# Routing of an attention and mixture-of-experts layer: counts by matmul from the picks, gates from sorted logits, a new order of steps, scatters waited for by the users of their buffers

## The chip, the cores and the metric

The kernel runs on one core of one Trainium2 chip. The metric is the device time of one execution in microseconds. A core has TensorE (PE, matmuls; PEld are its weight loads), VectorE (DVE), ScalarE (ACT), GpSimd (POOL) and SyncE (SP, here only a queue that issues transfers), which run their own instruction streams and meet at semaphores.

## The reference, cut to what matters

```python
x = layernorm(x + attention(x, W_K, W_Q, W_V, W_O))     # x: 2048 x 512, 16 heads of 128
x = layernorm(x + ffn(x, ...))

def ffn(x, gate_w, w1, w2, w3, sw1, sw2, sw3):          # 64 experts, 352 wide, top 6, capacity 128
    logits = x @ gate_w.T
    scores = softmax(logits)
    gate_vals, idx = top_k(scores, 6)
    fe = idx.reshape(-1); ft = repeat(arange(N), 6)     # choices in order of tokens
    onehot = fe[:, None] == arange(64)[None, :]
    pos = cumsum(onehot, axis=0) - 1  taken at fe       # place within its expert
    keep = pos < 128                                    # over capacity: dropped
    ...                                                 # rows gathered by (expert, pos)
    h = silu(xe @ w1.T) * (xe @ w3.T);  ye = h @ w2.T
    routed = sum over the 6 choices of ye * gate_val * keep
    z = (silu(x @ sw1.T) * (x @ sw3.T)) @ sw2.T         # shared expert
    return routed + z
```

## The kernel before, in words

The kernel has three parts, one after the other. `attention` works on pairs of heads. `route_and_experts` first goes through 16 tiles of 128 tokens (the routing loop), then through the experts. `combine` does the last layernorm. The change is in the routing loop and in the few units that follow it (the lead).

Each engine has its own `step(i, k)` of the routing loop, k from 0 to 15, and three tiles are in flight. In step k TensorE projects tile k with the output weights (`project`, 16 heads by three matmuls of 512 columns into `o_ps`), turns tile k-1 (`turn_x1`, four transposes into `t_ps`), counts the choices of tile k-2 (`counts`, into `c_ps`) and makes the logits of tile k-1 (`logits`, into `l_ps`). `LATE = (12, 14)` says that the transposes come after 12 heads and the counts after 14. VectorE in step k adds the residual and normalises tile k-1 (`normalise`), picks the experts of tile k-2 from its logits (`choose`), splits the heads' output of tile k+1 into a high and a low part (`split_z`), makes gates (`route_gates`), splits the turned tile k-1 (`split_x1T`) and works out the rows in the experts' buffers (`places`). ScalarE does the square root, the exponentials, the high parts, and in its step also a piece of the shared expert's weights (`split_shared`). GpSimd, after `placed`, sends the 128 rows of a tile to the six chosen experts by six indirect transfers (`scatter`), waits for them all to land, and only then subtracts the low part of a shared weight piece (`split_shared`) and issues the load of the next (`load_shared`). SyncE loads the heads' output of tile k+2 into the one buffer `z_raw` once `z_lo` of tile k+1 is made.

Normalised rows live in four buffers `x1` (`NB = 4`), with the token number, the chosen experts and the gates in their last 15 columns; slots in two. `normalise` of tile k waits for the scatters of tile k-4, `places` of tile k for those of tile k-2, both by `rows_left`, which GpSimd raises.

After the loop come eight lead units of the shared expert (`lead_up`, `lead_down`), between which the last two tiles are counted and placed. SyncE waits for all scatters before it loads the first expert's rows. A `done(i, k)` is the count a semaphore has once tile k is through; `link` chains the small VectorE steps by waits on a semaphore.

Of the kernel before, what the change touches and what calls it, by code (L numbers as in the profile page):

```python
# [7 lines left out]
P = 128  # L8
# [42 lines left out]
NB = 4  # L51
# [639 lines left out]
def route_and_experts(nc, z_dram, w_o, gate_w, x_rows, w13, w2, s13, s2, sums_dram, x1T_parts, gathered_x):  # L691
# [4 lines left out]
    LATE = (12, 14)  # L696
# [75 lines left out]
    with ExitStack() as ctx:  # L772
# [23 lines left out]
        with ExitStack() as first:  # L796
# [8 lines left out]
            token = sb("token", [P, TILES], I32, first)  # L805
# [9 lines left out]
            top_e = sb("top_e", [P, 8], stack=first)  # L815
            idx = sb("idx", [P, 8], U32, first)
            pick = sb("pick", [P, TOPK, EXPERTS], stack=first)
            pick_pos = sb("pick_pos", [P, TOPK, EXPERTS], stack=first)
            chosen = sb("chosen", [P, EXPERTS], stack=first)
            chosen_bf = sb("chosen_bf", [P, EXPERTS], BF16, first)  # L820
            count = sb("count", [P, EXPERTS], stack=first)
            pos_all = sb("pos_all", [P, EXPERTS], stack=first)
# [7 lines left out]
            ones_bf = sb("ones_bf", [P, P], BF16, first)  # L830
# [26 lines left out]
        with ExitStack() as first:  # L857
            o_ps = ps("o_ps", [P, 2, DM], stack=first)
            t_ps = ps("t_ps", [P, DT * P], stack=first)
            l_ps = ps("l_ps", [P, EXPERTS], stack=first)  # L860
            c_ps = ps("c_ps", [P, 2, EXPERTS], stack=first)
# [42 lines left out]
        l_read = sem("l_read")  # L904
        exp_ready = sem("exp_ready")
# [4 lines left out]
        moved = sem("moved")  # L910
        rows_left = sem("rows_left")
# [29 lines left out]
        LN_STEPS = 9  # L941
        CHOOSE_STEPS, GATE_STEPS = 6, 4
        ROUTE_STEPS = CHOOSE_STEPS + GATE_STEPS + 5
# [9 lines left out]
        def lead_turn(v):  # L953

            return NT - (LEAD - 1) + v

# [22 lines left out]
        def _(pool):  # L979
# [3 lines left out]
            nc.gpsimd.iota(token[:], pattern=[[P, TILES]], base=0, channel_multiplier=1).then_inc(pool_const, 1)  # L983
            pool.wait_ge(pool_step, 2)
# [4 lines left out]
                                    base=0, pattern=[[1, P]], channel_multiplier=-1).then_inc(pool_const, 1)  # L989
            nc.gpsimd.iota(mine_i[:], pattern=[[1, NE]], base=0, channel_multiplier=0).then_inc(pool_const, 1)  # L990
# [81 lines left out]
        def _(sp):  # L1072
# [88 lines left out]
            sp.wait_ge(rows_left, TILES)  # L1161
# [869 lines left out]
```

## Time and profile before

| what | value |
|---|---|
| median of 3 runs | 2573.56 us (2564.14 to 2576.12) |
| the profiled execution's own time | 2573.61 us |
| its span | 2571.8 us |
| TensorE busy | 2444.0 us, 95% |
| VectorE busy | 1778.3 us, 69% |
| ScalarE busy | 1423.4 us, 55% |
| GpSimd busy | 339.3 us, 13% |
| mean granted TensorE clock | 0.983 |

The span runs from the first to the last instruction. The shares are means over attention, routing loop, experts and final layernorm, which have different limits. The routing loop takes about the stretch from 1636 to 1869 us, the lead to about 1907 us. A row of the windows view gives start and end of a stretch and its length, the busy time (and count of instructions) of PE, PEld, DVE, ACT and POOL in it, then TensorE's granted clock as a share of 2.4 GHz, the DMA share and GB/s.

### The profile page before, as it was taken

The numbers are of one execution on the slowest core, as the hardware profiler recorded it, in microseconds if no ns is written. First come the engines' busy times: TensorE is split into PE (matmuls) and PEld (weight loads), VectorE is DVE, ScalarE is ACT, GpSimd is POOL, SyncE is SP. The second block draws the span as 40 slices with busy tenths as digits, with TensorE's granted clock in tenths as the row PEclk, the third lists the DMA queues.
The fourth block names the chain that finished last, engine by engine and source line by source line (L and its number), as shares of the span: only waits on it lengthen the run. The fifth ranks groups of instructions, "written<-read, shape, count | busy, mean of one in ns | idle before, by whom it ended". The sixth has DMA issues, their size and how long they took to land. (4 is left out here: it accounts for less than half of the span.)

```text
span 2571.8 us, 40617 instructions
## 1 busy us (share of the span) xinstructions
PE 2444.0 (95%) x14048; PEld 2115.2 (82%) x14048; DVE 1778.3 (69%) x3802; ACT 1423.4 (55%) x3183; POOL 339.3 (13%) x349
## 2 busy tenths in 40 slices
PE   6999999999999999999999999798899999999992
PEld 5888888888888888888888887677689898888992
DVE  4666666566566567567567657588868888788885
ACT  3555555455455456456446446444437777677771
POOL 0000000000000000000000000155541121212121
PEclk9999999999999999999999999899999999999996
DMA  6411411421421330431421321577659999999995
GB/s 260 132 62 56 139 58 60 134 62 48 134 71 28 130 99 24 125 104 28 126 89 42 104 67 30 195 250 265 221 149 315 297 300 314 284 296 310 310 303 153
DMA packets 193419, 396.99 MB, mean 154 GB/s; under 512 B 23673, under 2 KB 73209, under 8 KB 182976
## 3 DMA queue, kind: packets, MB, share of 16 engines
q1 hardware_dynamic: 163456, 330.69, 38.2%
q0 software_dynamic: 27456, 59.51, 10.0%
q10 hardware_dynamic: 2304, 4.20, 0.4%
q8 instruction: 113, 1.85, 0.3%
q14 instruction: 90, 0.74, 0.1%
HBM read 296.45 MB, written 106.48 MB: 157 GB/s over the span
## 5 line engine op out<-in xcount | busy, mean ns | idle before, releaser
L428 ACT ACTIVATE pT_hi<-turned 128x512 fp32r<-128x512 f32 (+3 forms) x640 | 334.1, 535 | 270.7 <-PE turned L638 268.2
L417 ACT ACTIVATE probs<-bank,neg_max 128x512 f32<-128x512 f32 (+3 forms) x640 | 396.6, 626 | 109.5 <-DVE neg_max L506 104.5
L512 DVE TENSOR_TENSOR pT_lo<-turned,pT_hi 128x512 fp32r<-128x512 f32 (+3 forms) x640 | 377.6, 603 | 75.0 <-ACT pT_hi L428 71.5
L498 DVE TENSOR_REDUCE max_part<-bank 128x1 f32<-128x512 f32 (+2 forms) x576 | 345.4, 620 | 95.9 <-PE bank L621 83.9
L608 PE MATMUL bank<-x_sb,w_hi 128*128 128x512 f32 x1024 | 323.9, 398 | 20.0 <-ACT ident_bf L393 13.3
L638 PE MATMUL turned<-ident,probs 128*128 128x128 f32 x2176 | 329.2, 273 | 0.1
L638 PEld LDWEIGHTS turned<-ident,probs 128*128 128x128 f32 x2176 | 264.2, 141 | 49.2 <-PE bank L597 0.3
L653 PE MATMUL z_ps<-pT_hi,v_hi 128*128 128x512 f32 (+3 forms) x640 | 255.0, 398 | 2.5 <-DVE pT_lo L512 2.0
L621 PE MATMUL bank<-k_lo,q_hi 128*128 128x512 f32 (+2 forms) x640 | 254.3, 397 | 0.0
L621 PE MATMUL bank<-k_hi,q_hi 128*128 128x512 f32 (+2 forms) x640 | 253.3, 396 | 0.0
L1739 DVE TENSOR_TENSOR up_lo<-w_raw,up_hi 128x704 fp32r<-128x704 f32 x256 | 217.4, 887 | 44.3 <-ACT up_hi L1246 40.4
L608 PEld LDWEIGHTS bank<-x_sb,w_hi 128*128 128x128 f32 x1024 | 190.1, 190 | 57.6 <-issue 13.2
L621 PE MATMUL bank<-k_hi,q_lo 128*128 128x512 f32 (+2 forms) x640 | 233.7, 365 | 0.0
L653 PE MATMUL z_ps<-pT_hi,v_lo 128*128 128x512 f32 (+3 forms) x640 | 233.7, 365 | 0.0
L653 PE MATMUL z_ps<-pT_lo,v_hi 128*128 128x512 f32 (+3 forms) x640 | 233.2, 364 | 0.0
L283 POOL DMA_DIRECT2D inv_dram<-inv x64 | 34.9, 546 | 1350.7 <-DVE inv L524 1350.7
L608 PE MATMUL bank<-x_sb,w_lo 128*128 128x512 f32 x512 | 201.1, 393 | 0.0
L597 PE MATMUL bank<-w_hi,x_sb 128*128 128x256 f32 x1024 | 193.8, 285 | 1.7 <-ACT probs L417 1.7
L1246 ACT ACTIVATE up_hi<-w_raw 128x704 fp32r<-128x704 f32 x250 | 185.5, 786 | 4.3 <-DMA w_raw<-in_w 3.8
L597 PEld LDWEIGHTS bank<-w_hi,x_sb 128*128 128x128 f32 x1024 | 164.1, 193 | 3.9 <-DVE probs L471 2.1
L1052 POOL DMA_INDIRECT sums_dram<-y_sb,token x64 | 112.5, 1759 | 395.2 <-DMA sums_dram<-y_sb,token 260.8
L597 PE MATMUL bank<-w_lo,x_sb 128*128 128x256 f32 x512 | 145.5, 284 | 0.0
(210 smaller groups left out, 5185.1 us busy)
## 6 DMA issues: line engine op xcount, KB each, us to landing
w_raw<-in_w SPq DMA_DIRECT2D x256, 352.0 KB
x_sb<-x_parts SPq DMA_DIRECT2D x62, 1024.0 KB, 6.2
w_raw<-in_w SPq DMA_DIRECT2D x128, 256.0 KB
rows_in<-gathered_x SPq DMA_DIRECT2D x64, 263.5 KB
spread_sb<-inv_dram POOLq DMA_DIRECT2D x64, 256.0 KB, 3.5
z_dram<-z_sb SPq DMA_DIRECT2D x64, 256.0 KB, 2.3
z_raw<-z_dram SPq DMA_DIRECT2D x16, 1024.0 KB
w_raw<-in_w_qkv SPq DMA_DIRECT2D x32, 384.0 KB, 8.6
```

What stands on the lines that cost most here:

```text
L417: nc.scalar.activation(probs[:, u % 2, r, kc * CHUNK:kc * CHUNK + used], bank[:, job_at["s", h, c, r, kc] % BANKS, 0:used], ACT.Exp, bias= ...
L428: nc.scalar.activation(pT_sb[0][:, n % TURNS, lo_col:], turned[:, n % TURNS, lo_col:], ACT.Copy).then_inc(turn_hi, 1)
L498: nc.vector.reduce_max(max_part[:, row % ROWS, kc:kc + 1], bank[:, job % BANKS, 0:used], axis=AX_X).then_inc(part_done, 1)
L512: nc.vector.tensor_tensor(pT_sb[1][:, n % TURNS, lo_col:], turned[:, n % TURNS, lo_col:], pT_sb[0][:, n % TURNS, lo_col:].bitcast(F32), AL ...
L597: mark = nc.tensor.matmul(dst[:, t * 2 * DH:(t + 1) * 2 * DH], x_sb[:, a, dt, rows_], w_sb[b][:, dt, 4 * DH:], start=(dt == 0 and (a, b) = ...
L608: mark = nc.tensor.matmul(dst, w_sb[a][:, dt, first:first + DH], x_sb[:, b, dt, :], start=(dt == 0 and (a, b) == PASSES[0]), stop=(dt == D ...
L621: mark = nc.tensor.matmul(dst[:, 0:width], q_sb[a][:, h, r * P:(r + 1) * P], k_sb[b][:, h, kc * CHUNK:kc * CHUNK + width], start=(a, b) == ...
L638: mark = nc.tensor.transpose(turned[:, n % TURNS, r * P:(r + 1) * P], probs[:, u % 2, r, j * P:(j + 1) * P], ident[:])
L653: mark = nc.tensor.matmul(z_ps[:, first * P:], v_sb[a][:, j, h * DH:(h + 1) * DH], pT_sb[b][:, n % TURNS, first * P:], start=(j == 0 and ( ...
L1052: nc.gpsimd.indirect_dma_start(sums_dram, bass.IndirectOffsetOnAxis(ap=token4[:, n:n + 1], axis=0), y_sb[:, n % 2], None, bounds_check=las ...
L1246: nc.scalar.activation(dst_of(0, n % 2, p, up_w, down_w), raw_of(raw, q % SLOTS_RAW, p), ACT.Copy).then_inc(w_hi, 1)
L1739: nc.vector.tensor_tensor(dst_of(1, n % 2, p, up_w, down_w), raw_of(raw, q % SLOTS_RAW, p), dst_of(0, n % 2, p, up_w, down_w).bitcast(F32) ...
```

## The change

- Counts. Before, VectorE summed the one-hot picks over the six choices, cast the sum to bf16, and kept a running `count` from a matmul with ones. Now `pick` is bf16 in two buffers; TensorE takes each of its six 64-column parts by itself into one open accumulation in `c_ps`: six matmuls with `rest_bf` that complete the tile before (over all its tokens), then six with `before_bf` (the tokens in front of each token). VectorE reads the places out of `c_ps` straight away.
- Gates. ScalarE takes the exponentials of the six sorted logits (`top`), in place of VectorE's product of `pick` with all 64 exponentials and its sum.
- The token number is written by a GpSimd iota into the row, not by a VectorE copy.
- The Newton step takes three instructions in place of five.
- Order. VectorE: the first half of the old `normalise` is `measure`; then `choose`, then the second half, `split_z`, gates, places, and last `split_x1T`. TensorE counts after 9 heads, and turns after 12. ScalarE splits the shared weight piece before it copies the turned tile.
- Scatters raise `rows_left[k % 2]` themselves; GpSimd doesn't wait for them, while VectorE, ScalarE and SyncE wait on the two new semaphores where they waited before.

```diff
-    LATE = (12, 14)
+    COUNTED, TURNED = 9, 12
...
             def scatter(k):
+                if k >= NB:
+                    pool.wait_ge(x1_stored[k % NB], 16 * (k // NB))
                 wait_apart(pool, waited, placed, done(0, k))
+                nc.gpsimd.iota(x1[:, k % NB, TOKEN:TOKEN + 1].bitcast(I32), pattern=[[0, 1]], base=k * P,
+                               channel_multiplier=1).then_inc(token_made, 1)
+                pool.wait_ge(token_made, k + 1)
                 for n in range(TOPK):
                     nc.gpsimd.indirect_dma_start(
                         flat, bass.IndirectOffsetOnAxis(ap=slot[:, k % 2, n:n + 1], axis=0), x1[:, k % NB], None,
-                        bounds_check=last_slot, oob_is_err=False).then_inc(moved, 16)
-                pool.wait_ge(moved, done(0, k, 16 * TOPK))
-                pool.sem_inc(rows_left, 1)
+                        bounds_check=last_slot, oob_is_err=False).then_inc(rows_left[k % 2], 16)
...
             def exponentials(i, k):
-                act.wait_ge(l_read, done(i, k))
-                nc.scalar.activation(ex[:], lg_c[:], ACT.Exp, accum_out=small[:, 4:5]).then_inc(exp_ready, 1)
+
+                act.wait_ge(topped, done(i, k))
+                nc.scalar.activation(ex[:], lg_c[:], ACT.Exp, accum_out=small[:, 4:5])
+                nc.scalar.activation(top_e[:], top[:, 0:TOPK], ACT.Exp).then_inc(exp_ready, 1)
...
                 if exists(i, k + 1):
                     split_z(i, k + 1)
+                if k < SHARED_PARTS * NP:
+                    split_shared(k)
                 if exists(i, k - 1):
                     turned_x1(i, k - 1)
-                if k < SHARED_PARTS * NP:
-                    split_shared(k)
...
             def counts(i, k):
-                pe.wait_ge(chosen_ready, done(i, k))
+
+
                 if exists(i, k - 1):
                     pe.wait_ge(c_read, done(i, k - 1))
-                nc.tensor.matmul(c_ps[:, 0], before_bf[:], chosen_bf[:], start=True, stop=True)
-                nc.tensor.matmul(c_ps[:, 1], ones_bf[:], chosen_bf[:], start=True, stop=True).then_inc(c_ready, 1)
+                    for n in range(TOPK):
+                        nc.tensor.matmul(c_ps[:], rest_bf[:], pick[:, (k - 1) % 2, n], start=False, stop=False,
+                                         skip_group_check=True)
+                pe.wait_ge(chosen_ready, done(i, k))
+                for n in range(TOPK):
+                    mark = nc.tensor.matmul(c_ps[:], before_bf[:], pick[:, k % 2, n], start=not exists(i, k - 1) and n == 0,
+                                            stop=n == TOPK - 1, skip_group_check=True)
+                mark.then_inc(c_ready, 1)
...
-                link(nc.vector.reduce_sum(chosen[:], pick[:].rearrange("p k e -> p e k"), axis=AX_X))
-                nc.vector.tensor_copy(chosen_bf[:], chosen[:]).then_inc(chosen_ready, 1)
...
-                link(nc.vector.tensor_tensor(pick_pos[:], pick[:], ex[:].rearrange("p (k e) -> p k e", k=1)
-                                             .to_broadcast([P, TOPK, EXPERTS]), ALU.mult))
-                link(nc.vector.reduce_sum(top_e[:, 0:TOPK], pick_pos[:], axis=AX_X))
...
-                link(nc.vector.tensor_tensor(pos_all[:], c_ps[:, 0], count[:], ALU.add))
-                nc.vector.tensor_tensor(count[:], c_ps[:, 1], count[:], ALU.add).then_inc(c_read, 1)
...
+                nc.vector.tensor_tensor(pick_pos[:], pick[:, k % 2], c_ps[:].rearrange("p (k e) -> p k e", k=1)
+                                        .to_broadcast([P, TOPK, EXPERTS]), ALU.mult).then_inc(c_read, 1)
```

On VectorE one step of the routing loop stood so before, from the statistics of a tile to the last instruction ahead of the next step (x is a buffer of `x1`, small the buffer of per-token values):

```order
L1612 BN_STATS stats<-x 128x6
...
L1619 TENSOR_SCALAR x<-x,mv,small 128x512
L1635 TENSOR_REDUCE small<-l_ps 128x1
...
L1643 TENSOR_TENSOR pick<-iota_f,x 128x384
L1647 TENSOR_REDUCE chosen<-pick 128x64
L1648 CAST chosen_bf<-chosen 128x64
L1597 TENSOR_TENSOR z_lo<-z_raw,z_hi 128x2048
L1655 TENSOR_TENSOR pick_pos<-pick,ex 128x384
L1657 TENSOR_REDUCE top_e<-pick_pos 128x6
```

The same place after the change:

```order
L1629 BN_STATS stats<-x 128x6
...
L1660 TENSOR_REDUCE small<-l_ps 128x1
...
L1672 TENSOR_TENSOR pick<-iota_f,x 128x384
L1638 RECIPROCAL small<-small 128x1
...
L1644 TENSOR_SCALAR x<-x,mv,small 128x512
L1614 TENSOR_TENSOR z_lo<-z_raw,z_hi 128x2048
L1685 RECIPROCAL small<-small 128x1
L1686 TENSOR_SCALAR x<-top_e,small 128x6
L1694 TENSOR_TENSOR pick_pos<-pick,c_ps 128x384
```

The picks now stand ahead of the normalised tile, nothing stands between them and the counts, and the instructions that summed over experts are gone.

On TensorE the end of a step's projection stood so before, with the transposes first:

```order
L1386 MATMUL t_ps<-ident,x 128x128 x4
L1374 MATMUL o_ps<-wo_hi,z_hi 128x512
...
L1374 MATMUL o_ps<-wo_hi,z_lo 128x512
L1393 MATMUL c_ps<-chosen_bf,before_bf 128x64
L1394 MATMUL c_ps<-chosen_bf,ones_bf 128x64
L1374 MATMUL o_ps<-wo_hi,z_hi 128x512
```

and after the change with the counts first, nine matmuls of the projection between the two, and twelve after the transposes:

```order
L1406 MATMUL c_ps<-pick,rest_bf 128x64 x6
L1410 MATMUL c_ps<-pick,before_bf 128x64 x6
L1385 MATMUL o_ps<-wo_hi,z_hi 128x512
...
L1385 MATMUL o_ps<-wo_hi,z_lo 128x512
L1397 MATMUL t_ps<-ident,x 128x128 x4
L1385 MATMUL o_ps<-wo_hi,z_hi 128x512
```

Twelve small matmuls stand where there were two, and they moved five heads ahead.

## Rows read from the trace of the kernel before

**Rows 1.** Windows: thirteen routing steps; the lead; the experts.
```profile
1661.97:1857.07 195.10, 175.55 (x833) 141.35 (x832) 168.30 (x442) 86.30 (x116) 107.79 (x95) 0.97 0.70 245
1868.84:1907.30 38.46, 37.67 (x227) 35.20 (x228) 27.17 (x77) 17.14 (x34) 21.40 (x20) 1.00 0.37 120
1960.00:2526.00 566.00, 549.95 (x3206) 505.21 (x3205) 461.40 (x913) 404.83 (x781) 117.12 (x72) 1.00 0.97 294
```

**Rows 2.** Timeline of DVE: residual adds of tiles 1 and 15.
```profile
1661.97 0.69 DVE L1610 TENSOR_TENSOR x<-o_ps,xr 128x512 f32<-128x512 f32 x1 [0.93 <-PE o_ps L1374]
1868.84 0.69 DVE L1610 TENSOR_TENSOR x<-o_ps,xr 128x512 f32<-128x512 f32 x1 [0.34 <-issue]
```

**Rows 3.** Waits from 1661.97 to 1868.84: total us, times, longest.
```profile
PE c_ps L1393 <- DVE chosen_bf L1648: 13.5, 9, 2.4
...
DVE x L1610 <- PE o_ps L1374: 0.9, 1, 0.9
```

**Rows 4.** Timeline of PE: a step's start, its counts, the next step's start.
```profile
1662.58 0.48 PE L1374 MATMUL o_ps<-wo_hi,z_hi 128*128 128x512 f32 x1
...
1672.69 0.20 PE L1393 MATMUL c_ps<-chosen_bf,before_bf 128*128 128x64 bf16 x1
1672.73 0.19 PE L1394 MATMUL c_ps<-chosen_bf,ones_bf 128*128 128x64 bf16 x1
...
1673.07 0.39 PE L1374 MATMUL o_ps<-wo_lo,z_hi 128*128 128x512 f32 x1
...
1675.03 0.48 PE L1374 MATMUL o_ps<-wo_hi,z_hi 128*128 128x512 f32 x1
```

**Rows 5.** Timeline of DVE: places in one step that the change touches.
```profile
1784.16 0.17 DVE L1616 RECIPROCAL small<-small 128x1 f32<-128x1 f32 x1 [0.43 <-ACT small L1197]
...
1785.32 0.55 DVE L1619 TENSOR_SCALAR x<-x,mv,small 128x512 f32<-128x512 f32 x1
...
1787.97 0.85 DVE L1647 TENSOR_REDUCE chosen<-pick 128x64 f32<-128x384 f32 x1
...
1788.96 2.29 DVE L1597 TENSOR_TENSOR z_lo<-z_raw,z_hi 128x2048 fp32r<-128x2048 f32 x1
1791.17 0.55 DVE L1655 TENSOR_TENSOR pick_pos<-pick,ex 128x384 f32<-128x384 f32 x1
...
1792.34 0.16 DVE L1658 RECIPROCAL small<-small 128x1 f32<-128x1 f32 x1
...
1793.96 0.21 DVE L1668 TENSOR_TENSOR pos_all<-c_ps,count 128x64 f32<-128x64 f32 x1
...
1794.35 0.55 DVE L1670 TENSOR_TENSOR pick_pos<-pick,pos_all 128x384 f32<-128x384 f32 x1
```

**Rows 6.** Timeline of POOL: first scatter, shared split, next tile's first scatter.
```profile
1776.12 1.93 POOL L1010 DMA_INDIRECT gathered_x<-x,slot  x1 [0.30 <-issue]
...
1791.31 1.98 POOL L1004 TENSOR_TENSOR s_up_lo<-s_raw,s_up_hi 128x704 fp32r<-128x704 f32 x1 [6.82 <-DMA gathered_x<-x,slot]
...
1794.48 1.29 POOL L1010 DMA_INDIRECT gathered_x<-x,slot  x1 [0.30 <-issue]
```

**Rows 7.** Timelines of DVE, SP and ACT: two loads of z_raw.
```profile
1647.91 2.29 DVE L1597 TENSOR_TENSOR z_lo<-z_raw,z_hi 128x2048 fp32r<-128x2048 f32 x1 [2.08 <-ACT z_hi L1192]
...
1655.23 1.92 ACT L1192 ACTIVATE z_hi<-z_raw 128x2048 fp32r<-128x2048 f32 x1 [2.85 <-DMA z_raw<-z_dram]
...
1777.21 0.32 SPq L1074 DMA_DIRECT2D z_raw<-z_dram  x1
...
1786.61 1.90 ACT L1192 ACTIVATE z_hi<-z_raw 128x2048 fp32r<-128x2048 f32 x1
```

**Rows 8.** Timelines of POOL and ACT: a shared piece's load, its use.
```profile
1761.95 0.59 POOL L999 DMA_DIRECT2D s_raw<-in_s  x1 [0.30 <-POOL s_up_lo L1004]
...
1766.18 0.79 ACT L1221 ACTIVATE s_up_hi<-s_raw 128x704 fp32r<-128x704 f32 x1 [7.87 <-DMA s_raw<-in_s]
```

**Rows 9.** Timeline of SP: the first expert's rows, after all scatters.
```profile
1907.34 0.32 SPq L1162 DMA_DIRECT2D rows_in<-gathered_x  x1
```

More of the change, by code:

```diff
@@ L860, in route_and_experts @@
             l_ps = ps("l_ps", [P, EXPERTS], stack=first)
-            c_ps = ps("c_ps", [P, 2, EXPERTS], stack=first)
+            c_ps = ps("c_ps", [P, EXPERTS], stack=first)
         h_even = ps("h_even", [P, 2, CHUNK])
@@ L909, in route_and_experts @@
         placed = sem("placed")
-        moved = sem("moved")
-        rows_left = sem("rows_left")
+        rows_left = [sem(f"rows_left{n}") for n in range(2)]
+        token_made = sem("token_made")
         ln_chain = sem("ln_chain3")
@@ L982, in _ @@
             nc.gpsimd.iota(iota_i[:], pattern=[[1, EXPERTS]], base=0, channel_multiplier=0).then_inc(pool_const, 1)
[L983 to L984 removed]
+            nc.gpsimd.memset(rest_bf[:], 1.0).then_inc(pool_step, 1)
+            pool.wait_ge(pool_step, 3)
             nc.gpsimd.affine_select(out=ident[:], in_=ident[:], compare_op=ALU.not_equal, fill=1.0,
@@ L1160, in _ @@
             load_tile(3, 1)
-            sp.wait_ge(rows_left, TILES)
+            for m in range(2):
+                sp.wait_ge(rows_left[m], rows_of(TILES - 2 + m))
             sp.dma_start(rows_in[:, 0], gathered_x[0]).then_inc(rows_loaded[0], 16)
@@ L1252, in split_first @@
                 if n % 2:
-                    act.wait_ge(rows_left, TILES)
+                    for m in range(2):
+                        act.wait_ge(rows_left[m], rows_of(TILES - 2 + m))
                     for m in range(NB):
@@ L1405, in step @@
                 if exists(i, k):
-                    project(i, k, range(0, LATE[0]))
+                    project(i, k, range(0, COUNTED))
+                if exists(i, k - 2):
+                    counts(i, k - 2)
+                if exists(i, k):
+                    project(i, k, range(COUNTED, TURNED))
                 if exists(i, k - 1):
@@ L1409, in step @@
                 if exists(i, k):
-                    project(i, k, range(LATE[0], LATE[1]))
-                if exists(i, k - 2):
-                    counts(i, k - 2)
-                if exists(i, k):
-                    project(i, k, range(LATE[1], HEADS))
+                    project(i, k, range(TURNED, HEADS))
                 if exists(i, k - 1):
@@ L1598, in split_z, with measure @@
                                         ALU.subtract).then_inc(z_lo, 1)
-            def normalise(i, k):
+            def measure(i, k):
                 link = chained(ln_chain, i, k, LN_STEPS, 0)
@@ L1686, in step @@
                 if exists(i, k - 1):
-                    normalise(i, k - 1)
+                    measure(i, k - 1)
                 if exists(i, k - 2):
                     choose(i, k - 2)
+                if exists(i, k - 1):
+                    normalise(i, k - 1)
                 if exists(i, k + 1):
```

82 lines of the change are left out of this document (40 added, 42 removed).

## The prediction

> **What bounds the kernel now.** The page's shares say that TensorE is busy 95% of the whole, so I first looked for the stage in which the changed code stands and asked there who waits for whom. The windows view of thirteen routing steps shows TensorE 175.55 us busy of 195.10, VectorE 168.30 [rows 1]: neither is full, and the granted clock is 0.97, not 1. The timeline of VectorE gives the pace: its first instruction of a step, the residual add, starts at 1661.97 us for tile 1 and at 1868.84 for tile 15 [rows 2], that is 206.87 us for 14 steps, 14.78 us each. In that stretch VectorE's add waited for the projection once, for 0.9 us, while TensorE waited nine times, 13.5 us in all, for the cast picks [rows 3]. So VectorE, which goes from one step into the next without a wait for TensorE, sets the pace; its idle share is in the gaps between chained small instructions.
>
> What TensorE could do by itself is seen where nothing held it. The step that starts at 1662.58 ends where the next starts, at 1675.03: 12.45 us with 48 projection matmuls, four transposes, logits and two counting matmuls [rows 4]. So 14.78 - 12.45 = 2.33 us of each step are to be had from VectorE before TensorE stops the gain.
>
> **The change part by part, VectorE.** I take start to start, so that the gap behind an instruction counts with it, all in one step [rows 5].
> - Sum over choices and cast: 1787.97 to 1788.96, 0.99 us gone.
> - Picks times exponentials, and their sum: 1791.17 to 1792.34, 1.17 us gone.
> - Adding the running count, twice: 1793.96 to 1794.35, 0.39 us gone. The product now reads `c_ps` itself. The trace has no product of this size out of PSUM; below it is the 0.55 us of the same product from SBUF, above it 0.69 us, the residual add, which reads PSUM at a third more columns. At most 0.14 us comes back; I take 0.05.
> - Newton: from the reciprocal to the normalising instruction 1.16 us for six starts, so 0.19 each; two fewer, 0.38 us.
> - The wait for the square root, 0.43 us, is covered: `choose` now stands between the variance and the reciprocal, and takes longer than ScalarE's root does.
> - The token copy ran beside its neighbours; I count nothing. It becomes an iota on GpSimd.
>
> Sum 0.99 + 1.17 + 0.39 - 0.05 + 0.38 + 0.43 = 3.31 us. VectorE alone would come down to 14.78 - 3.31 = 11.5 us a step, which is below 12.45: VectorE stops being the bound, and the gain is cut by TensorE.
>
> **TensorE.** Ten more counting matmuls each step. Two stood between the projection's matmuls at 1672.69 and 1672.73, and the second projection matmul after them starts at 1673.07. With 0.23 us for each of those, the two cost 1673.07 - 0.23 - 1672.69 = 0.15 us [rows 4]. From start to start they are 0.04 us apart; that is the lower price of one more, 0.4 us for ten. The upper one comes from the logits, eight records of 64 columns in f32 between 1674.2 and 1675.03, so 0.10 us each, 1.0 us for ten. The new ones are bf16 of the same shape as the two, so I stay near the lower end: 0.055 us each, 0.55 us. A step then takes 12.45 + 0.55 = 13.0 us.
>
> The Trainium skill, "TensorE: Matmul & The Clock Gate", section "LDWEIGHTS (loading the stationary operand)", gives columns / 1.2 in ns, 107 ns for 128 columns; this is the rule that speaks most against spelling one sum out in twelve matmuls. By it alone the step would be 12.45 + 1.07 = 13.5 us. The pair in the trace, 0.04 us apart, does not bear it out, since the loads run ahead.
>
> Do TensorE's feeds come in time at 13 us? With T the start of VectorE's step, which is the end of the projection before, TensorE starts its own step 0.8 us later (the logits). `measure` takes about 2.0 us (the add 0.69 [rows 2], the statistics about as long over as many columns, two small ones), and `choose` up to the picks at most the 2.65 us from 1785.32 to 1787.97 [rows 5], in which the normalising instruction lies too. So the picks are complete at T + 4.6 at the latest, and wanted after nine heads of three matmuls at 0.23 us, T + 0.8 + 6.2 = T + 7.0. The second half of `normalise` takes 1.16 - 0.38 + 0.55 = 1.3 us: the normalised tile is ready at T + 5.9 and wanted three heads later, at T + 9.7. `z_lo` takes 2.2 us more (1788.96 to 1791.17), with a short wait for ScalarE T + 8.6, and is wanted at T + 13.8. Each has over 2 us to spare, so the waits for the picks go, and with TensorE no longer idle I expect the clock of these steps at 1.0.
>
> **GpSimd.** It leaves out the wait for landing, 6.82 us in the row. What is left in its cycle is the issue of six scatters, 1776.12 to 1784.49, 8.37 us, and split, load and start of the next, 1791.31 to 1794.48, 3.17 us [rows 6]. With a short iota, 11.9 us: below 13.0. The old wait itself cost the pace nothing (VectorE didn't wait for it), but its old cycle, 18.4 us in this tile, would have been in the way of a faster pace; that is what this part buys. Who waits in its place: VectorE, for scatters of two tiles before (at `places`) and four tiles before. `places` ends at about T + 11, issue at T + 19.5, landing 7 us later at T + 26.5; the slots are used again two steps later in the same place, T + 37. Covered by 10 us.
>
> **ScalarE.** One small activation more, under the 1.9 us of `split_z` in front of the copies; ScalarE is busy 86.30 of 195.10 us [rows 1]. Nothing.
>
> **Queues.** SyncE's order is untouched. In the lead, TensorE is busy 37.67 of 38.46 us [rows 1], so VectorE's savings bring nothing there, and the last two counts add 2 x 0.55 = 1.1 us. The first expert's rows are loaded at 1907.34 [rows 9], after the last scatter; GpSimd's shorter backlog moves this forward, no later. The experts run with TensorE at 549.95 of 566 us [rows 1] and keep their length.
>
> **Sum.** 206.87 - 14 x 13.0 = 24.9 us less in the loop, 1.1 more in the lead: 23.8. The profiled execution took 2573.61 us, and the median is 2573.56, the same. 2573.6 - 23.8 = 2549.8; I say 2550.
>
> **The rivals.**
> - *Dear counts.* Each small matmul shows its weight load, 0.10 us: the step is 13.5 us, the loop saves 206.9 - 189 = 17.9, the lead loses 2.0, which gives 2557.7. For it: the upper row. Against it: the pair 0.04 apart. The skill's rule above is this case. 10%.
> - *VectorE still sets the pace.* Its stalls move, and its step waits for ScalarE: `split_z` stands 3 us earlier, and the last `split_x1T` now waits for ScalarE's copy at about T + 11.2. If that makes 13.5 to 14, the time is 2557 to 2563. Against it: 11.5 us leave 1.5 us of slack. 8%.
> - *The load of `z_raw`.* One buffer: load, 1.9 us on ScalarE, 2.3 on VectorE, with waits some 4.5 us besides the load. An undisturbed load took from 1650.20 to 1655.23, 5.0 us; in the loop 9.4 us from issue to use brought no wait [rows 7]. Between these the landing is unknown. From 8.5 us on this chain is longer than 13.0; at 9.4 a step is 13.9, and 206.9 - 194.6 = 12.3 gives 2562. DMA share goes from 0.70 to about 0.8. 8%.
> - *Slower: the shared piece behind the scatters.* `load_shared` now goes into GpSimd's queue behind scatters that haven't landed, and ScalarE waits for the piece ahead of `turned_x1`, which TensorE's logits wait for. The piece was in use 4.2 us after its issue [rows 8], with the scatters gone. The cycle is its landing + 0.8 (ScalarE) + 2.0 + 0.9 (split, issue). Above 11.1 us to land it exceeds 14.78 and the kernel is slower: at 13 us it is 16.7 and the time 2600. Added to the 4.2 us, the 6.8 us for which a whole tile's scatters were waited come to 11.0, just below; yet some 2 us of split pass before the issue. 4%.
> - *More than forecast.* Counts at 0.035 and scatters' end some 5 us earlier against the lead, which lets the experts' loads start earlier: 2542. 7%.
>
> **How the numbers follow.** The forecast has 63%, with a range of its own of 2544 to 2556 (a step of 12.7 to 13.4 us). Cases between the named ones lie within. To hold 8 in 10 the range reaches to the dear counts and to the slower loads at one end and the extra gain at the other: 2542 to 2563. A measurement tells 0.5%, 12.9 us, from no change, so below 2560.7 counts as faster: forecast, extra gain, dear counts and most of the VectorE case, 86%. Within 0.5%: the `z_raw` case and the rest of these, 10%. Slower: 4%.
>
> **What the profile after would show.** Residual adds 13.0 us apart, each waiting 1 to 2 us for `o_ps`; no wait of TensorE on picks; the twelve counting matmuls within 0.8 us; GpSimd waiting for places rather than for landing; clock 1.0. It is wrong if TensorE waits at the logits (copy behind the shared piece), at the start of a projection (`z_lo`), or if the twelve matmuls take over a microsecond.

## The result, and the profile after

| | kernel before | changed kernel |
|---|---|---|
| median, 5 runs each on the same chip | 2567.18 us (2564.14 to 2576.12) | 2544.89 us (2539.08 to 2550.91) |
| profiled execution, its span | 2573.61, 2571.8 us | 2545.8, 2543.9 us |
| VectorE busy | 1778.3 us | 1738.1 us |
| TensorE busy | 2444.0 us | 2438.9 us |

The ratio is 0.990, 95% interval 0.9881 to 0.9919: faster by 22.3 us by the medians, where 23.8 was forecast against a profiled execution. The two profiled executions differ by 27.8 us.

The windows of the changed kernel, for the 14 steps from tile 1's to tile 15's residual add and for the first 39 us of the lead:

```profile
1661.45:1839.99 178.54, 178.54 (x1005) 147.63 (x1003) 143.20 (x349) 92.19 (x137) 124.00 (x117) 1.00 0.78 278
1839.99:1879.00 39.01, 39.01 (x259) 36.95 (x258) 22.46 (x61) 17.29 (x35) 19.28 (x20) 1.00 0.46 138
```

TensorE is busy in all of the 178.54 us and its clock stands at 1.00, that is 2.4 GHz; in [rows 1] it had gaps and 0.97. VectorE is busy 143.20 of 178.54. The loop is 206.87 - 178.54 = 28.3 us shorter [rows 2], 12.75 us a step for 14.78. The span is 27.9 us shorter, so by VectorE's adds all of the gain is in these 14 steps.

VectorE's timeline, two residual adds with what the change touches between them, the last add of the loop, and one small instruction that comes up below:

```profile
1811.56 0.54 DVE L1698 TENSOR_SCALAR full<-pos 128x6 f32<-128x6 f32 x1
...
1814.45 0.69 DVE L1627 TENSOR_TENSOR x<-o_ps,xr 128x512 f32<-128x512 f32 x1 [0.96 <-PE o_ps L1385]
...
1818.27 0.56 DVE L1672 TENSOR_TENSOR pick<-iota_f,x 128x384 bf16<-128x384 f32 x1
...
1820.31 2.29 DVE L1614 TENSOR_TENSOR z_lo<-z_raw,z_hi 128x2048 fp32r<-128x2048 f32 x1
...
1822.98 0.56 DVE L1694 TENSOR_TENSOR pick_pos<-pick,c_ps 128x384 f32<-128x384 bf16 x1
...
1825.57 0.69 DVE L1651 TENSOR_TENSOR x1T_lo<-t_ps,x1T_hi 128x512 fp32r<-128x512 f32 x1 [0.72 <-ACT x1T_hi L1223]
...
1827.22 0.69 DVE L1627 TENSOR_TENSOR x<-o_ps,xr 128x512 f32<-128x512 f32 x1 [0.96 <-PE o_ps L1385]
...
1839.99 0.69 DVE L1627 TENSOR_TENSOR x<-o_ps,xr 128x512 f32<-128x512 f32 x1 [0.95 <-PE o_ps L1385]
```

With T = 1814.45 the picks are complete at T + 4.4 (T + 4.6 was forecast) and the next tile's `z_lo` at T + 8.2 (T + 8.6). The step of 12.77 us holds 0.72 + 0.96 us of waits, so VectorE's own chain (its instructions and the gaps between them, without the waits for other engines) is 11.1 us here, for 11.5 forecast. But this is a step in which GpSimd splits no shared piece. In the 14 steps VectorE waits 7.9 + 3.1 + 1.4 us for other engines (the waits below), which leaves (178.5 - 12.4) / 14 = 11.9 us a step for its own chain; in the steps with a split it is 11.5 to 12.75 us, since one small instruction, such as the one at 1811.56, takes 0.35 to 1.3 us longer than elsewhere. The product out of PSUM takes 0.56 us; the 0.05 us taken for it was not there.

TensorE's timeline around the counts:

```profile
1782.80 0.39 PE L1385 MATMUL o_ps<-wo_hi,z_lo 128*128 128x512 f32 x1
1783.03 0.35 PE L1406 MATMUL c_ps<-pick,rest_bf 128*128 128x64 bf16 x6
1783.22 0.34 PE L1410 MATMUL c_ps<-pick,before_bf 128*128 128x64 bf16 x6
1783.39 0.48 PE L1385 MATMUL o_ps<-wo_hi,z_hi 128*128 128x512 f32 x1
1783.71 0.40 PE L1385 MATMUL o_ps<-wo_lo,z_hi 128*128 128x512 f32 x1
```

From the first count to the second projection matmul behind them are 1783.71 - 1783.03 = 0.68 us; less the 0.23 of one projection matmul, twelve counts cost 0.45 us, for 0.15 us for two [rows 4]. Ten more cost 0.30 us, 0.03 each.

The waits in the loop, 1661.45 to 1839.99 (total us, times, longest):

```profile
POOL x L1015 <- issue: 13.5, 7, 3.9
DVE x L1627 <- PE o_ps L1385: 7.9, 13, 1.0
...
POOL x L1015 <- DVEq L1705: 3.9, 3, 1.3
...
DVE x1T_lo L1651 <- ACT x1T_hi L1223: 3.1, 4, 1.8
...
DVE pick_pos L1694 <- PE c_ps L1410: 1.4, 1, 1.4
```

Against [rows 3]: TensorE no longer waits for picks (it has no wait for data at all here), and VectorE waits for the projection 13 times in place of once. GpSimd waits ahead of its iota and never for landing. The view names no releaser for 13.5 us of it, but the iota at 1800.63 below starts 0.2 us after VectorE's last instruction of the places (1800.24, 0.17 us long): it is the places that it waits for. GpSimd's timeline from one shared split to the next, then one instruction of VectorE's beside it:

```profile
1795.57 2.67 POOL L1008 TENSOR_TENSOR s_down_lo<-s_raw,s_down_hi 128x512 fp32r<-128x512 f32 x1
1798.54 0.58 POOL L1003 DMA_DIRECT2D s_raw<-in_s  x1 [0.29 <-POOL s_down_lo L1008]
1800.63 0.12 POOL L1015 IOTA x<- 128x1 int32 x1 [1.51 <-issue]
1801.29 1.02 POOL L1019 DMA_INDIRECT gathered_x<-x,slot  x1 [0.53 <-POOL x L1015]
...
1807.76 3.00 POOL L1019 DMA_INDIRECT gathered_x<-x,slot  x1 [0.30 <-issue]
1810.76 1.31 POOL L1008 TENSOR_TENSOR s_down_lo<-s_raw,s_down_hi 96x512 fp32r<-96x512 f32 x1
```
```profile
1807.63 2.28 DVE L1614 TENSOR_TENSOR z_lo<-z_raw,z_hi 128x2048 fp32r<-128x2048 f32 x1
```

The split stands straight behind the sixth scatter, where [rows 6] show 6.82 us of waiting. From split to split are 15.2 us in this tile, 1.51 of them idle: 13.7 us of work with a sixth scatter that takes 3.00, and 11.7 with one of 1.0, for 11.9 forecast. The long sixth scatter starts 0.13 us after VectorE's `z_lo` and ends 0.85 us after it; so do all five scatters over 1.3 us in this loop. GpSimd's idle time in other tiles takes up the difference.

### The profile page after: what moved, and what is told of

Read it like the earlier page. It is cut to its first block and busy times, and to the rows that moved or that the text cites. A ratio compares the mean times of both kernels' runs of the same rounds, so it can differ in the third digit from the quotient of the medians.

```text
span 2543.9 us, 40857 instructions
## 1 busy us (share of the span) xinstructions
PE 2438.9 (96%) x14202; PEld 2117.1 (83%) x14202; DVE 1738.1 (68%) x3656; ACT 1425.4 (56%) x3199; POOL 346.6 (14%) x366
```

## The experiments

"Steps" below is the time from tile 1's to tile 15's residual add, divided by 14. Each kernel was timed in five rounds against the kernel before; the ratios are to that kernel. The steps are read from one profiled execution each. They tell more than its whole time: behind the lead's last wait of TensorE (for `ys_sb`), where all these kernels do the same work, the profiled executions spread from 645.6 us (experiment 1) to 660.4 us (experiment 2).

**1. The wait put back, all the rest changed.**

```diff
                         bounds_check=last_slot, oob_is_err=False).then_inc(rows_left[k % 2], 16)
+                pool.wait_ge(rows_left[k % 2], rows_of(k))
```

> The changed kernel with one thing undone: GpSimd waits again for the landing of a tile's six scatters before it goes on. Theory: GpSimd's own cycle was a second bound, hidden behind VectorE's. In the trace of before its first scatters of tiles 1 and 11 start 1697.00 and 1850.36 us, 15.3 us apart per tile, and it never waited for the places but once. So with the wait back, VectorE waits for the scatters, the loop goes at 14 to 15.3 us a tile instead of 12.77, and the kernel takes 2563 to 2573 us, as before or nearly. Rival: the wait lay beside other work and cost nothing, since VectorE never waited for scatters before; then 2545 us and 12.8 us a step.

Measured: 2569.72 us, ratio 0.9987 (0.997 to 1.0004); steps of 14.42 us, uneven (12.6 to 17.1), in the profiled execution, which with 2560.48 us was the fastest of twelve. By the median the whole gain is gone. Its timelines of POOL, ACT and PE, in this order, one fence each:

```profile
1779.17 0.98 POOL L1019 DMA_INDIRECT gathered_x<-x,slot  x1 [0.30 <-issue]
1783.72 3.44 POOL L1008 TENSOR_TENSOR s_up_lo<-s_raw,s_up_hi 128x704 fp32r<-128x704 f32 x1 [3.57 <-DMA gathered_x<-x,slot]
1787.45 0.59 POOL L1003 DMA_DIRECT2D s_raw<-in_s  x1 [0.30 <-POOL s_up_lo L1008]
1788.06 0.15 POOL L1015 IOTA x<- 128x1 int32 x1
```
```profile
1791.54 0.79 ACT L1232 ACTIVATE s_up_hi<-s_raw 128x704 fp32r<-128x704 f32 x1 [8.27 <-DMA s_raw<-in_s]
1792.24 0.58 ACT L1219 ACTIVATE x1T<-t_ps 128x512 f32<-128x512 f32 x1
```
```profile
1792.87 1.10 PE L1420 MATMUL l_ps<-gw,x1T 128*128 128x64 f32 x8 [1.83 <-ACT x1T L1219]
```

Read across: GpSimd waits 3.57 us for landing, splits, loads the next piece at 1787.45 and starts the next tile at once (its iota has no idle time: the places had long been there). The piece lands in time for ScalarE only at 1791.54; ScalarE, in order, makes the copy of the turned tile behind it; TensorE's logits wait for that. So GpSimd's cycle, 14 to 18 us from first scatter to first scatter in the first nine tiles, is the bound, and it reaches TensorE through a load and ScalarE's order. ScalarE waits for shared pieces 61.7 us in the loop. The time is as expected, the way is not: VectorE, which was expected to wait for the scatters, doesn't wait for them once. This is the mechanism of the prediction's slower rival, in a kernel where the wait stands.

**2. The wait alone removed from the kernel before**, with the two semaphores and the waits that go with them, nothing else.

```diff
-                        bounds_check=last_slot, oob_is_err=False).then_inc(moved, 16)
-                pool.wait_ge(moved, done(0, k, 16 * TOPK))
-                pool.sem_inc(rows_left, 1)
+                        bounds_check=last_slot, oob_is_err=False).then_inc(rows_left[k % 2], 16)
```

> The kernel before with only GpSimd's wait for the landing taken away (the scatters raise two semaphores, on which VectorE, ScalarE and SyncE wait in the old places); VectorE's work and all orders are the old ones. Theory: VectorE's chain sets 14.8 us a step by itself, so nothing is gained: 2562 to 2570 us against 2567. Rival: the wait was the bound all along (GpSimd never waited for the places), then the step falls to below 14 us and the time to 2550 to 2557.

Measured: 2577.65 us, ratio 1.0009 (0.9991 to 1.0027); steps of 15.09 us for 14.78. Taking the wait away is worth nothing at the old pace, and by experiment 1 the whole gain at the new one: neither part gives anything without the other. Experiments 8 and 9 narrow down what the wait does.

**3. The old order of steps on TensorE (shown), VectorE (`normalise` before `choose`, `split_x1T` before `places`) and ScalarE (the shared piece last), all the rest changed.**

```diff
-                    project(i, k, range(0, COUNTED))
+                    project(i, k, range(0, 12))
+                if exists(i, k - 1):
+                    turn_x1(i, k - 1)
+                if exists(i, k):
+                    project(i, k, range(12, 14))
...
-                    project(i, k, range(COUNTED, TURNED))
-                if exists(i, k - 1):
-                    turn_x1(i, k - 1)
-                if exists(i, k):
-                    project(i, k, range(TURNED, HEADS))
+                    project(i, k, range(14, HEADS))
```

> The changed kernel with the old order of steps on VectorE, TensorE and ScalarE (normalise whole, then choose; x1T split ahead of the places; transposes after 12 heads and counts after 14; shared piece after the turned tile). Theory: the order only gives slack; with VectorE's chain at 11.1 us and the picks ready at about T + 4.9, the old places still have 2 us and more, so 2545 to 2549 us, of which the wait for the root returning to VectorE (0.4 us a step) is within its slack. Rival: the order is part of the gain, since the wait for the root and the split behind ScalarE's copy bring VectorE's step over 12.77; then 13.2 us a step and 2551 us or more.

Measured: 2541.54 us, ratio 0.9876 (0.9852 to 0.9899); steps of 12.80 us for 12.75. The order is worth nothing here: in that window TensorE is busy 179.18 us of 179.18, so both orders feed it in time. The time is below the 2545 to 2549 us expected, level with the changed kernel within the intervals. In this order VectorE waits again for the square root, 0.43 us in each of the 14 steps, as the prediction had read it, and the pace doesn't change: this saving is slack too.

**4. 24 more counting matmuls in each step**, whose results nobody reads.

```diff
+                for n in range(24):
+                    mark = nc.tensor.matmul(c_ps[:, 1], before_bf[:], pick[:, k % 2, n % TOPK], start=False, stop=False,
+                                            skip_group_check=True)
```

> The changed kernel with 24 more matmuls of 64 columns in bf16 in each step, into a second part of c_ps that nobody reads. Theory: TensorE is the bound of the loop and a small matmul costs it 0.03 us, so 0.72 us a step, 16 steps, 11.5 us in all: 2556 us, and 13.5 us from one residual add to the next. Rival 1: VectorE is the bound; then the added matmuls vanish in TensorE's idle time, 2545 us. Rival 2: a small matmul shows its weight load, 0.055 to 0.1 us: 2566 to 2583 us.

Measured: 2556.99 us, ratio 0.9934 (0.9909 to 0.9959). Its window of the loop and, from TensorE's timeline, the counts of a step:

```profile
1662.88:1851.22 188.34, 188.34 (x1341) 157.45 (x1339) 146.17 (x350) 92.20 (x137) 124.49 (x117) 1.00 0.74 264
```
```profile
1790.76 0.35 PE L1406 MATMUL c_ps<-pick,rest_bf 128*128 128x64 bf16 x6
1790.94 0.34 PE L1410 MATMUL c_ps<-pick,before_bf 128*128 128x64 bf16 x6
1791.12 0.86 PE L1413 MATMUL c_ps<-pick,before_bf 128*128 128x64 bf16 x24
```

188.34 - 178.54 = 9.8 us for 14 x 24 matmuls is 0.029 us each, and VectorE waits for the projection ahead of every add: the step is TensorE's, and each small matmul lengthens it by its price.

**5. The old gates** (picks times exponentials and their sum) back on VectorE.

```diff
-                nc.scalar.activation(top_e[:], top[:, 0:TOPK], ACT.Exp).then_inc(exp_ready, 1)
...
+                link(nc.vector.tensor_tensor(pick_pos[:], pick[:, k % 2], ex[:].rearrange("p (k e) -> p k e", k=1)
+                                             .to_broadcast([P, TOPK, EXPERTS]), ALU.mult))
+                link(nc.vector.reduce_sum(top_e[:], pick_pos[:], axis=AX_X))
```

> The changed kernel with the gates made the old way (VectorE multiplies the picks by all 64 exponentials and sums; ScalarE's second activation gone). Theory: TensorE is the bound at 12.77 us a step, VectorE's chain in the changed kernel is 11.1 us and grows by 1.17 us to 12.3, so most steps stay at 12.8 and only those in which VectorE is held up grow: 2544 to 2550 us. Rival: the gates' 1.17 us are on the path; then 13.9 us a step and 2560 us.

Measured: 2548.12 us, ratio 0.9904 (0.9878 to 0.9931). The window:

```profile
1660.51:1842.67 182.16, 180.00 (x1005) 148.08 (x1003) 158.26 (x377) 90.82 (x123) 122.07 (x116) 1.00 0.78 272
```

13.01 us a step, and VectorE waits for the projection once, for 0.9 us: it is the bound again. The time is in the expected range, but ten of the 14 steps take 12.98 to 13.40 us where most were expected at 12.8. The expectation built on the 11.1 us of the one step without a split; from the mean of 11.9 the sum is 11.9 + 1.17 = 13.1.

**6. Counts from one mask**: one comparison of the logits with the sixth largest gives the sum over the choices; two counting matmuls, none of the twelve.

```diff
-                    for n in range(TOPK):
-                        nc.tensor.matmul(c_ps[:], rest_bf[:], pick[:, (k - 1) % 2, n], start=False, stop=False,
-                                         skip_group_check=True)
+                    nc.tensor.matmul(c_ps[:], rest_bf[:], mask[:, (k - 1) % 2], start=False, stop=False,
+                                     skip_group_check=True)
...
+                nc.vector.tensor_scalar(mask[:, k % 2], lg_c[:], top[:, TOPK - 1:TOPK], None, ALU.is_ge
+                                        ).then_inc(chosen_ready, 1)
```

> The changed kernel with the counts made from one mask: VectorE compares the 64 logits with the sixth largest (one instruction, a bf16 one-hot sum over the choices at once, which is equal to the sum of the six picks where no two logits are equal), and TensorE multiplies rest_bf and before_bf by it, two matmuls in place of twelve. Theory: TensorE is the bound and ten small matmuls cost 0.03 us each, so a step goes from 12.77 to 12.47 us and the time falls by 16 x 0.3 = 4.8 us to about 2540 us; VectorE's chain grows from 11.1 to 11.4. Rival: VectorE holds the loop already; then 2545 us or more.

Measured: 2541.3 us, ratio 0.9881 (0.9852 to 0.991). The window:

```profile
1662.32:1837.06 174.74, 174.74 (x870) 143.72 (x868) 144.48 (x364) 92.18 (x137) 125.92 (x117) 1.00 0.80 284
```

12.48 us a step with TensorE full: this is the 12.45 us that the prediction read off one undisturbed step of the kernel before [rows 4].

**7. The sum over the choices and its cast back on VectorE**, with two counting matmuls.

```diff
+                link(nc.vector.reduce_sum(chosen[:], pick[:, k % 2].rearrange("p k e -> p e k"), axis=AX_X))
+                nc.vector.tensor_copy(mask[:, k % 2], chosen[:]).then_inc(chosen_ready, 1)
```

> The changed kernel with the sum over the six choices back on VectorE (reduction and cast to bf16, 0.99 us) and two counting matmuls in place of twelve, in the same accumulation. Theory: VectorE's chain grows to 12.1 us and stays below TensorE's 12.47, so the sum on VectorE costs nothing any more once the gates and the wait are gone: 2540 to 2546 us. Rival: moving the sum was needed; then VectorE sets about 13.1 us a step and 2550 us or more.

Measured: 2540.99 us, ratio 0.9884 (0.9856 to 0.9912). The window:

```profile
1661.46:1838.25 176.79, 175.26 (x870) 143.96 (x868) 153.44 (x378) 92.19 (x137) 132.10 (x117) 1.00 0.78 281
```

VectorE waited for the projection once: at 12.63 us a step it is just the bound again, and still the step is shorter than the changed kernel's, since TensorE is rid of ten matmuls. One step of 14.45 us stands out: its `z_lo` at 1756.92 takes 4.50 us in place of 2.29, with GpSimd's split beside it from 1757.53 to 1759.26. Without those 2.2 us the mean is 12.47.

**8. The wait put back, with ScalarE's shared piece behind the copy of the turned tile.**

```diff
+                pool.wait_ge(rows_left[k % 2], rows_of(k))
...
-                if k < SHARED_PARTS * NP:
-                    split_shared(k)
                 if exists(i, k - 1):
                     turned_x1(i, k - 1)
+                if k < SHARED_PARTS * NP:
+                    split_shared(k)
```

> The changed kernel with GpSimd's wait for the landing back, as in the first run of this study, and with the shared piece split after the turned tile on ScalarE, as before. In that run TensorE waited for the logits behind ScalarE, which waited 61.7 us in all for the shared pieces that GpSimd loads late. Theory: the late piece is what the wait costs; with the old ScalarE order it holds up only ScalarE's next root, and VectorE goes at 12.8 us until it is two tiles ahead of GpSimd, whose cycle of 16.5 us (first scatters of tiles 0 to 7 in that run) then sets the pace through the slots: 14 to 15 us a step on the mean, 2562 to 2574 us. Rival: only the ScalarE order made the wait dear; then 12.8 us a step and 2545 to 2550 us.

Measured: 2555.99 us, ratio 0.9947 (0.9927 to 0.9967); steps of 13.45 us. That lies between the two expectations, 2562 to 2574 and 2545 to 2550. About half of the wait's price was ScalarE's order, so the one-cause reading of experiment 1 was too narrow. Three rows of its waits, 1662 to 1860, show the rest:

```profile
ACT s_up_hi L1232 <- DMA s_raw<-in_s: 29.4, 4, 8.5
...
DVE z_lo L1615 <- ACT z_hi L1201: 15.8, 9, 2.2
PEld c_ps L1411 <- DVE pick L1673: 8.9, 7, 2.1
```

ScalarE still stands at the late piece, and now `z_hi` of the next step and with it VectorE's `z_lo` come late.

**9. The wait put back, but behind the split and the next load.**

```diff
             def scatter(k):
+                if k:
+                    pool.wait_ge(rows_left[(k - 1) % 2], rows_of(k - 1))
```

> The changed kernel, but GpSimd waits again until the scatters of each tile have landed; the wait stands behind the split and the load of the next shared piece, ahead of the next tile's scatters, where the first experiment had it ahead of both. Every tile's landing is waited for, as before. My theory: what the wait costs depends on what stands behind it. In the first two experiments with the wait it was a shared piece that came late to ScalarE, and a GpSimd cycle of 14.2 to 16.5 us. Here the 3 us or so of split and load issue lie under the landing, so the cycle is six scatters, 8.4 us, and a landing of some 4 to 6 us behind the last, 12.5 to 14, and the piece is asked for as early as in the changed kernel. I expect steps of 12.8 to 13.3 us and 2545 to 2553 us. The rival: the wait costs by itself, wherever it stands; then the time is that of the first experiment, 2560 to 2575. No cost at all would be 2545.

Measured: 2550.03 us, ratio 0.9894 (0.9874 to 0.9914). Its window, two rows of GpSimd's timeline and one of its waits in the loop:

```profile
1661.56:1842.13 180.57, 179.12 (x1005) 147.45 (x1004) 145.49 (x350) 92.70 (x137) 109.86 (x112) 1.00 0.79 274
```
```profile
1757.01 0.60 POOL L1003 DMA_DIRECT2D s_raw<-in_s  x1 [0.30 <-POOL s_up_lo L1008]
1760.87 0.12 POOL L1017 IOTA x<- 128x1 int32 x1 [3.27 <-DMA gathered_x<-x,slot]
```
```profile
POOL x L1017 <- DMA gathered_x<-x,slot: 33.1, 12, 4.4
```

GpSimd waits for landing as before, 3.27 us here and 33.1 us in twelve waits over the loop, and the steps stay at 12.90 us. So it was not the wait that cost the time in experiment 1, but what stood behind it. The changed kernel would have had its gain, within the intervals, with the wait kept and moved.

**10. Both pieces of work (5 and 7) back on VectorE**, the wait still away. Besides the line shown, the edit is that of 5 and 7 together.

```diff
-        CHOOSE_STEPS, GATE_STEPS = 4, 2
+        CHOOSE_STEPS, GATE_STEPS = 5, 4
```

> The changed kernel with both pieces of work back on VectorE: the sum over the choices with its cast (two counting matmuls), and picks times exponentials with their sum. GpSimd's wait stays away, and the new order of steps stays. My theory: apart, each fitted under TensorE's 12.5 us; together they don't, since VectorE's own work comes to 11.1 + 0.99 + 1.17 = 13.3 us, and the small instructions that are held up while GpSimd splits add some tenths. I expect steps of 13.3 to 13.8 us, no wait of VectorE for the projection, and 14 x 0.8 = 11 us more than the changed kernel: 2552 to 2560. The rival: the gain came from the wait and the order, and VectorE's instructions were never the bound; then steps stay at 12.5 to 12.8 us and the time at 2541 to 2546. A third: the whole gain was VectorE's work, and then this comes within 0.3% of the kernel before.

Measured: 2560.1 us, ratio 0.9944 (0.9926 to 0.9962). Its window, then from its timelines of POOL and DVE one shared split and two small instructions:

```profile
1661.01:1853.80 192.79, 177.02 (x870) 144.59 (x869) 170.26 (x406) 90.92 (x123) 132.06 (x116) 1.00 0.73 258
```
```profile
1783.56 1.71 POOL L1010 TENSOR_TENSOR s_up_lo<-s_raw,s_up_hi 128x704 fp32r<-128x704 f32 x1
```
```profile
1783.78 0.16 DVE L1685 RECIPROCAL small<-small 128x1 f32<-128x1 f32 x1
1783.98 1.33 DVE L1686 TENSOR_SCALAR x<-top_e,small 128x6 f32<-128x6 f32 x1
```

13.77 us a step with no wait for the projection: VectorE is the bound. The sum 11.1 + 0.99 + 1.17 = 13.3 us lacks 0.5, and that last row can cover it: six elements a partition take 1.33 us and end at 1785.31, where GpSimd's split ends (1785.27). In 11 steps it takes 0.9 or 1.3 us in place of 0.2, 0.7 us for the mean step.

**11. That instruction with two tensor inputs instead of one.**

```diff
-                link(nc.vector.tensor_scalar(x1[:, k % NB, GATES:GATES + TOPK], top_e[:], small[:, 5:6], None, ALU.mult))
+                link(nc.vector.tensor_tensor(x1[:, k % NB, GATES:GATES + TOPK], top_e[:],
+                                             small[:, 5:6].to_broadcast([P, TOPK]), ALU.mult))
```

> The kernel of the experiment before (both pieces of work back on VectorE, whose steps take 13.77 us with VectorE as the bound), with one instruction in another form: the six exponentials times the reciprocal of their sum. It was an instruction with one tensor and a scalar per token (128x6); now it has two tensors, the second the same scalar read six times. In the trace of that kernel this instruction takes 0.92 or 1.33 us in 11 of the steps instead of 0.23, and ends each time as GpSimd's subtraction of a shared piece ends (started 0.42 to 0.44 us before it, 1.3 or 1.7 us long). My theory: an instruction with one tensor input is held back while GpSimd's two-input subtraction runs, one with two inputs isn't. Then the instruction takes about 0.2 us in every step, the loop loses five times 0.7 and six times 1.1 us, about 10 us, steps take 13.0 us, and the time is 2548 to 2553. The rival: any small VectorE instruction behind the start of the subtraction is held back, whatever its form; then it still takes 0.9 or 1.3 us, and the time stays at 2557 to 2563. A third: the hold moves to the next instruction with one tensor input, 2.2 us later, where a subtraction of 1.3 to 1.7 us has ended; that would again be 2557 to 2563, with another instruction at 0.9 us.

Measured: 2560.27 us, ratio 0.9948 (0.9929 to 0.9968), steps of 13.76 us. One split and the instruction, from the timelines of POOL and DVE:

```profile
1784.37 1.72 POOL L1010 TENSOR_TENSOR s_up_lo<-s_raw,s_up_hi 128x704 fp32r<-128x704 f32 x1
```
```profile
1784.80 1.33 DVE L1686 TENSOR_TENSOR x<-top_e,small 128x6 f32<-128x6 f32 x1
```

My theory on the form fell: the instruction is held back in the same way with two inputs. That the hold has to do with the split is seen by the two ends falling together in all 11 steps. Not every instruction is held: the reciprocal at 1783.78 in experiment 10, 0.2 us after the split's start, takes its usual 0.16 us. By what they exclude each other was not settled.

## Why the prediction came out as it did

**Pace and bound: right.** VectorE set 14.78 us and TensorE took over. That the medians' 22.3 us stand so close to the forecast 23.8 is in part luck: the kernel before came out 6.4 us lower in this comparison (2567.18 us) than in the one that the forecast started from, and profile against profile the gain is 27.8 us, 4 more than forecast. Most of these 4 us are one term, the price of the counts below. Experiments 5, 7 and 10 give the limits in one table, steps and ratio to before:

| | sum over choices by TensorE | sum on VectorE |
|---|---|---|
| gates by ScalarE | 12.75 us, 0.9900 | 12.63 us, 0.9884 |
| gates on VectorE | 13.01 us, 0.9904 | 13.77 us, 0.9944 |

Down the left column TensorE gives way to VectorE by 0.26 us; in the right column it is 1.14. The savings on VectorE are worth their full price only until TensorE's 12.45 to 12.75 us is reached; from then on one of the two moves would have done. Alone, the move of the sum to TensorE brings nothing once the gates are gone: it frees VectorE time that nobody needs and costs TensorE 0.3 us a step (experiments 6 and 7).

**The counts: the step that was mis-sized.** The term of the sum that failed is the price of the ten more counts. The prediction took 0.055 us for each of ten, 0.55 us a step; they cost 0.30 us a step (timeline), 0.03 each, and 0.029 each in experiment 4. 14 x 0.25 = 3.5 us is nearly all of the difference between 24.9 and 28.3 us in the loop. I had stayed above the lower bound of 0.04, the distance of the pair [rows 4], because of the f32 logits; the bf16 counts follow the pair, and less. The rival of dear counts falls with it. The Trainium skill, "TensorE: Matmul & The Clock Gate", section "LDWEIGHTS (loading the stationary operand)", gives 107 ns for the load of 128 columns; as a price of one more matmul in a stream the trace doesn't bear it out: each count loads its own 128 columns (0.10 us by the load's own record) and the step grows by 30 ns.

**VectorE's parts: right one by one, their sum 0.4 us too good.** The product out of PSUM cost nothing extra, the wait for the root is worth its 0.43 us (experiment 3), and the feeds came 0.2 to 0.4 us before the forecast times. But VectorE's own chain is 11.9 us in the mean of the 14 steps for 11.5 forecast; only a step without a shared split has 11.1. What the prediction lacked is the hold: while GpSimd splits, a small VectorE instruction is held back, by 0.7 us in the mean step (`full` at 1811.56 with 0.54 us in place of 0.17, in seven steps the gates' instruction of line 1686 with 1.1 to 1.5 us in place of 0.23). In the changed kernel TensorE's step hides it; in experiments 5 and 10 it lies on the path. Newton's two instructions and the two adds of the running count were not tried one by one.

**GpSimd's wait: right in part.** That it cost the pace nothing is experiment 2; that its old cycle would have been in the way of a faster pace is experiment 1. The size of the old cycle, 18.4 us from one tile, was high: 14.4 us a step came out. What was not seen is that only the place of the wait matters: what hurt was the late load and, through it, ScalarE; with the wait behind that load the steps are only 0.14 us longer (experiment 9).

**The two loads: no wait.** `z_raw` never held the loop up. ScalarE waited for shared pieces 0.3 us in all; they landed 3.9 to 6.2 us after their issue, far from the 11.1 us at which the slower rival begins.

**Lead and experts.** From tile 15's add to the span's end it was 702.9 us and is 703.9, +1.0 for 1.1 forecast, and that is luck. From the add to the lead's last wait of TensorE (for `ys_sb`, ending at 1917.24 us before and at 1890.40 now) it is 2.0 us more: 48.4 and 50.4. About 0.6 of it are the twenty more counts at 0.03 us. The rest fits where the count starts: before, TensorE had started its last matmul of tile 15's projection 3.2 us ahead of VectorE's add (1865.63 and 1868.84), now 0.4 us (1839.56 and 1839.99); from that matmul on, the lead is 0.8 us shorter than before. Behind the lead it is 1.1 us less, far inside the spread of that part over all runs. Clock 1.00 in the loop as forecast; waits for `o_ps` of 0.2 to 1.0 us where 1 to 2 were forecast, since TensorE's step is shorter by 0.25 us and VectorE's chain longer by 0.4 us than forecast.

The order of steps, to which the prediction gave no price beyond the covered root, has none here while GpSimd doesn't wait (experiment 3). With the wait in its old place, ScalarE's new order costs about 1 us a step (experiments 1 and 8).

## What to carry to other kernels

Before shortening the engine that sets the pace, read from one undisturbed step what the next engine needs by itself: the gain stops there (12.45 us here, found again as 12.48 in experiment 6), and every further saving is spent on slack. A blocking wait in an in-order queue costs what stands behind it: put the work that others need ahead of it, or let those who need the result wait; test it at the new pace, since at the old one it can look free. When two edits each do nothing alone, as taking the wait away and the shorter chain do here (with ScalarE's new order; with the old one the shorter chain gives about half, experiment 8), a comparison that removes them one at a time from the changed kernel shows it, and one that adds them one at a time to the old kernel doesn't. The experiments point to versions with two counting matmuls (6 and 7, 2541 us), level with the changed kernel within the intervals and both below the kernel before.

## What the runs showed of the hardware

- Twelve bf16 matmuls of 64 columns, each with its own weight load, lengthen a stream of 512-column matmuls by 0.45 us; 24 more by 0.70 us, 0.029 each, at clock 1.00.
- A VectorE product of 384 elements takes 0.56 us with one input in PSUM, as long as from SBUF.
- While GpSimd subtracts two SBUF tensors (1.3 or 1.7 us), a VectorE instruction on 128x6 in SBUF that starts 0.4 us later takes 0.9 or 1.3 us in place of 0.2, and ends with it, with one tensor input or with two (experiments 10 and 11, 11 steps each). In the same stretches the reciprocal (0.16 us at 1783.78 of experiment 10), the reduction (0.55 us at 1810.86 of the changed kernel) and the product with one input in PSUM (0.54 us at 1695.92 of experiment 3) take their usual time. The cause was not tried.
- The other way round, an indirect scatter that starts on GpSimd while VectorE subtracts two 128x2048 SBUF tensors (`z_lo`, 2.3 us) takes 2.1 to 3.0 us in place of 1.0 in the changed kernel, and ends 0.85 us after that subtraction, five times of five; in experiment 10 it takes 3.0 us and ends 0.85 to 0.87 us after it, twelve times of twelve. This too is read from the traces and was not tried by an edit.
